# The lower levels of a block inverse in 32x32 tiles of the array, and FP4 weights decoded by their bits

## Time and profile before

| | us |
|---|---|
| three runs | 4791.87, 4797.97, 4799.29 (median 4797.97) |
| the profiled execution | 4795.44 |
| its span | 4793.6 |
| TensorE busy | 4570.4 (95%) |
| VectorE (DVE) busy | 3585.9 (75%) |
| ScalarE (ACT) busy | 2307.5 (48%) |
| POOL busy | 514.6 (11%) |

### The profile page before, as it was taken

One profiled execution on the slowest core, in us unless ns is written; L12 is line 12 of the kernel. 1 busy time (PEld: TensorE's weight loads), 2 busy tenths in 40 slices (PEclk: granted clock), 3 DMA queues, 4 the chain that ended last, 5 costly groups with the idle time before them and its releaser, 6 DMA issues. The chain is left out here.

```text
span 4793.6 us, 61029 instructions
## 1 busy us (share of the span) xinstructions
PE 4570.4 (95%) x20341; PEld 2909.4 (61%) x20341; DVE 3585.9 (75%) x8682; ACT 2307.5 (48%) x4841; POOL 514.6 (11%) x381
## 2 busy tenths in 40 slices
PE   7899999999999999999999999998577999999899
PEld 4677777677777677777677777667333444444343
DVE  5777777777777777777777777776475988988861
ACT  4455454555554555554554554553223554555433
POOL 1111111111111111111111111111010000000000
PEclk9999999999999999999999999999889999999999
DMA  2010110111100111100110100100200444444420
GB/s 75 31 34 32 35 33 27 34 32 29 38 30 27 34 33 58 43 29 27 34 34 27 38 29 27 34 27 10 83 1 18 161 144 136 156 145 145 150 90 18
DMA packets 202330, 262.10 MB, mean 55 GB/s; under 512 B 18174, under 2 KB 101378, under 8 KB 202018
## 3 DMA queue, kind: packets, MB, share of 16 engines
q1 hardware_dynamic: 202018, 258.20, 16.9%
HBM read 249.24 MB, written 8.91 MB: 54 GB/s over the span
## 5 line engine op out<-in xcount | busy, mean ns | idle before, releaser
L436 PE MATMUL bank<-xnT,w_qkv 128*128 128x512 f32 x2048 | 925.1, 594 | 4.1 <-ACT raw L720 3.4
L436 PEld LDWEIGHTS bank<-xnT,w_qkv 128*128 128x128 f32 x2048 | 373.5, 191 | 401.9 <-issue 383.2
L1004 DVE SCALAR_TENSOR_TENSOR conv<-raw,conv_w,conv 128x1024 f32<-128x1024 f32 x384 | 496.1, 1292 | 154.8 <-ACT conv L694 145.7
L547 PE MATMUL bank<-w_out_unit,oT 128*128 128x512 f32 x1024 | 497.1, 608 | 7.9 <-ACT oT L760 7.9
L508 PE MATMUL bank<-w_z_unit,xnT 128*128 128x256 f32 x2048 | 486.8, 381 | 0.0
L508 PEld LDWEIGHTS bank<-w_z_unit,xnT 128*128 128x128 f32 x2048 | 371.2, 191 | 41.2 <-issue 1.0
L791 ACT ACTIVATE squares<-o 128x128 f32<-128x128 f32 x512 | 153.9, 301 | 454.9 <-DVE o L1048 392.8
L1211 PE MATMUL bank<-xnT_f,w_gu 128*128 128x512 f32 x704 | 345.7, 637 | 11.1 <-PEq L1536 7.0
L1219 PE MATMUL bank<-xnT_f,w_gu 128*128 128x512 f32 x704 | 318.2, 595 | 0.0
L1229 PE MATMUL bank<-w_down,hidden 128*128 128x512 f32 x704 | 316.7, 593 | 1.1 <-DVE x_blocks L1271 1.1
L1103 POOL TENSOR_TENSOR inv<-n_base,block_mask 128x1024 f32<-128x1024 f32 x64 | 150.5, 2352 | 1422.2 <-DVE n_base L851 1422.2
(11 more groups left out here) (219 smaller groups left out, 8510.4 us busy)
## 6 DMA issues: line engine op xcount, KB each, us to landing
rows_b<-bc_rows SPq DMA_DIRECT2D x256, 256.0 KB, 3.3
rows_c<-bc_rows SPq DMA_DIRECT2D x256, 256.0 KB, 3.4
w_qkv<-in_w_qkv SPq DMA_DIRECT2D x128, 256.0 KB, 2.8
decay<-gc_rows SPq DMA_DIRECT2D x64, 512.0 KB, 3.9
w_z_unit<-in_w_z SPq DMA_DIRECT2D x32, 512.0 KB, 4.4
w_out_unit<-in_w_out SPq DMA_DIRECT2D x32, 512.0 KB, 5.0
x_after<-x SPq DMA_DIRECT2D x16, 256.0 KB, 2.0
x_blocks<-x_after SPq DMA_DIRECT2D x4, 1024.0 KB, 12.3
```

The source lines that it names most:

```text
L436: made = e.matmul(PROJ[:, :], w_qkv[:, p % 2, j, :], xnT[:, n // HK, j, h * BANK:(h + 1) * BANK], start=j == 0, stop=j == KT - 1)
L547: made = e.matmul(OB[:, :], oT[:, r, :], w_out[:, N % 2, r, :], start=r == 0, stop=r == REP - 1)
L1004: e.scalar_tensor_tensor(acc, raw[:, i % 2, tap:tap + T], conv_w[:, tap, col:col + 1], acc, ALU.mult, ALU.add).then_inc(on["conv"], 1)
```

## The change

The constants: the two masks `neg_mask` are gone; `slot_mask` (128 x 64) and `neg_odd` are made from `block_mask` by DVE.

`inv` is kept by rows of 64: a row of a matrix holds only the 64 columns of its own half (for rows 0 to 63 the columns 0 to 63, for rows 64 to 127 the columns 64 to 127). POOL's spread is 128 x 512. A tile `inv_turned` of the same shape holds the transposed squares before level 0.

```diff
+                for i in range(NC):
+                    if level == 0:
+                        for b in range(4):
+                            q, s = slice(32 * b, 32 * b + 32), 32 * (b % 2)
+                            if part == 0:
+                                made = e.matmul(evens_ps[q, i, :, :], lt[q, i, q], evens[q, i, :, :],
+                                                start=True, stop=True)
+                            else:
+                                made = e.matmul(tile_ps[q, i, :], inv_turned[q, i, s:s + 32], off[q, i, 0:32],
+                                                start=True, stop=True)
+                    elif level == 1:
+                        for b in range(2):
+                            up, low = slice(64 * b, 64 * b + 32), slice(64 * b + 32, 64 * b + 64)
+                            if part == 0:
+                                made = e.matmul(tile_ps[low, i, :], lt[up, i, low], inv[up, i, 0:32],
+                                                start=True, stop=True)
+                            else:
+                                made = e.matmul(tile_ps[up, i, :], off[low, i, 0:32], ttT[low, i, low],
+                                                start=True, stop=True)
+                        if part == 1:
+                            low = slice(32, 64)
+                            made = e.matmul(tile_ps[low, i, :], ttT[low, i, low], off[low, i, 0:32],
+                                            start=True, stop=True)
```

Level 2 keeps its 64 x 64 tiles. Part 0 of level 0 now waits for POOL's mask and not for DVE's transpose. DVE's side:

```diff
-            def turn_inverse(N, a):
-                ttT = invT_i(a)
-                e.transpose(ttT.rearrange("p n w -> p (n w)"), inv[:, :, :].rearrange("p n w -> p (n w)")).then_inc(
-                    on["inv_dve"], 1)
+            def turn_base():
+                e.transpose(inv_turned[:, :, :].rearrange("p n w -> p (n w)"),
+                            inv[:, :, :].rearrange("p n w -> p (n w)")).then_inc(on["inv_dve"], 1)
+
+            def turn_inverse(a):
+                for q in (slice(0, hp), slice(hp, P)):
+                    e.transpose(invT_i(a)[q, :, q], inv[q, :, :]).then_inc(on["inv_dve"], 1)
...
-                            mask = c["neg_mask"][16 << level][:, :].unsqueeze(1).broadcast_to([P, NC, P // 2])
-                            e.tensor_tensor(off[:, :, :], inv_ps, mask, ALU.mult).then_inc(on["inv_dve"], 1)
+                            sign = c["neg_odd"][:, 0:1] if level == 0 else -1.0
+                            e.tensor_scalar(off[:, :, 0:32], tile_ps, sign, None, ALU.mult).then_inc(on["inv_dve"], 1)
...
                             if level == 0:
+                                e.tensor_tensor(evens, evens_ps, evens, ALU.add).then_inc(on["inv_dve"], 1)
                                 e.wait_ge(on["inv_dve"], INV_STEPS * H + 3)
-                                turn_inverse(N, a)
+                                if n >= 1:
+                                    e.wait_ge(on["u_pe"], 8 * (n - 1) + HALF * a + HALF)
+                                turn_inverse(a)
                             else:
-                                e.wait_ge(on["inv_dve"], INV_STEPS * H + 6)
+                                e.tensor_copy(inv[32:64, :, 0:32], tile_ps[32:64, :, :]).then_inc(on["inv_dve"], 1)
                                 for q in (0, 64):
-                                    e.transpose(ttT[q:q + 32, :, q + 32:q + 64],
-                                                inv[q + 32:q + 64, :, q:q + 32]).then_inc(on["inv_dve"], 1)
+                                    e.tensor_copy(invT_i(a)[q:q + 32, :, q + 32:q + 64], tile_ps[q:q + 32, :, :]).then_inc(
+                                        on["inv_dve"], 1)
```

```diff
-                        e.tensor_scalar(spread[:, :, j], words, 4 * j, 15, ALU.logical_shift_right,
-                                        ALU.bitwise_and).then_inc(on["unpacked"], 1)
+                        e.tensor_scalar(spread[:, :, j], words, 4 * (NIB - 1 - j), 6, ALU.logical_shift_left,
+                                        ALU.arith_shift_right).then_inc(on["unpacked"], 1)
...
+                    e.tensor_scalar(bits, bits, FLOAT_BITS, None, ALU.bitwise_and).then_inc(on["unpacked"], 1)
                     e.wait_ge(on["unpacked"], done + NIB + 1)
...
+                    e.tensor_tensor(values.rearrange("p (g w) -> p g w", g=ng),
+                                    bits.bitcast(F32).rearrange("p (g w) -> p g w", g=ng),
+                                    by.unsqueeze(2).broadcast_to([P, ng, P]), ALU.mult).then_inc(on["unpacked"], 1)
```

```diff
+        def beside(i, place):
+
+            ahead = [("piece", k) for k in pieces_before(i + 1)] if i + 1 < IT else []
+            return (ahead[0:1], ahead[1:2], ahead[2:] + state_space[2 * (i - 2):2 * (i - 1)] if i >= 2 else ahead[2:])[place]
```

More of the change, by code:

```diff
@@ L149 @@
     gate x_add
-    pad select k_weight mask square o_scaled
+    pad inv_zero select k_weight mask square o_scaled
 """
@@ L347, in inverse @@
                 H = 2 * N + a
[L348 to L353, removed]
-                    else:
[L355 to L373, removed]
@@ new lines, in inverse @@
+                lt, ttT = lT_i[:, NC * a:NC * (a + 1), :], invT_i(a)
+                if level == 0 and part == 0:
+                    e.wait_ge(on["mask"], H + 1)
+                    if H > 0:
+                        e.wait_ge(on["invT"], H)
+                elif level < 2:
+                    e.wait_ge(on["inv_dve"], INV_STEPS * H + ((0, 2), (3, 6))[level][part])
+                elif part == 0:
+                    e.wait_ge(on["inv_dve"], INV_STEPS * H + 9)
+                else:
+                    e.wait_ge(on["inv_neg"], H + 1)
@@ new lines, in inverse @@
+                for i in range(NC):
[14 more added lines that the diff above has]
+                                                start=True, stop=True)
+                            else:
+                                made = e.matmul(tile_ps[up, i, :], off[low, i, 0:32], ttT[low, i, low],
[4 more added lines that the diff above has]
+                                            start=True, stop=True)
+                    elif part == 0:
+                        made = e.matmul(inv_ps[hp:P, i, :], lt[0:hp, i, hp:P], inv[0:hp, i, :],
+                                        start=True, stop=True)
+                    else:
+                        made = e.matmul(inv_ps[0:hp, i, :], off[hp:P, i, :], ttT[hp:P, i, hp:P],
+                                        start=True, stop=True)
@@ L1083, in gpsimd @@
             e.memset(raw[:, :, 0:PAD], 0.0).then_inc(on["pad"], 1)
+            e.memset(invT[:, :, :, 0:hp].rearrange("p c r w -> p (c r) w"), 0.0).then_inc(on["inv_zero"], 1)
             for slot in range(ATTENTION_SLOTS):
@@ L1137 @@
 BLOCKS = B * NH
+FLOAT_BITS = -0x7E400000
+HALF_POWER = 2.0 ** 63
 TILES = BANK // P
@@ L1315, in second_half @@
         order = [k for i in range(IT) for k in pieces_before(i)]
+        state_space = [("small", 0), ("dt_rows", 0)]
+        state_space += [("dt_w", i) for i in range(KT)] + [("out_w", i) for i in range(KT)]
+        def beside(i, place):
+            ahead = [("piece", k) for k in pieces_before(i + 1)] if i + 1 < IT else []
+            return (ahead[0:1], ahead[1:2], ahead[2:] + state_space[2 * (i - 2):2 * (i - 1)] if i >= 2 else ahead[2:])[place]
         prep = [("scale", 0), ("scale", 1)] + [("turn0", t) for t in range(TILES)]
-        prep += [("piece", k) for k in pieces_before(0)] + [("small", 0), ("dt_rows", 0)]
-        prep += [("dt_w", i) for i in range(KT)] + [("out_w", i) for i in range(KT)]
-        prep += [("piece", k) for i in range(1, IT) for k in pieces_before(i)] + [("turn1", t) for t in range(TILES)]
+        prep += [("piece", k) for k in pieces_before(0)]
+        prep += [use for i in range(IT) for place in range(3) for use in beside(i, place)]
+        prep += [("turn1", t) for t in range(TILES)]
         prep_at = {use: k for k, use in enumerate(prep)}
@@ L1398, in prepare @@
                         ng = piece(i)[1]
-                        e.wait_ge(on["scaled"], order.index(i) + 1)
+                        e.wait_ge(on["unpacked"], UNPACK_STEPS * (order.index(i) + 1))
                         values = val[:, order.index(i) % 2, 0:ng * P].rearrange("p (g w) -> p g w", g=ng)
@@ L1455, in scalar @@
                     evict(("turn0", t))
+                for k in pieces_before(0):
+                    evict(("piece", k))
                 for i in range(IT):
-                    for k in pieces_before(i):
-                        evict(("piece", k))
+                    for use in beside(i, 0):
+                        evict(use)
                     silu_gate(e, 0, i)
-                    if i == 0:
-                        for use in prep[prep_at[("small", 0)]:prep_at[("out_w", KT - 1)] + 1]:
-                            evict(use)
+                    if i == 2:
                         e.wait_ge(on["ss_params"], 48)
```

(17 more changed lines are left out.)

96 lines of the change are left out of this document (41 added, 55 removed).

## The result

The changed kernel takes 4494.0 us (median of four, 4491.8 to 4494.4) where the kernel before takes 4795.3; the ratio is 0.937, 95% interval 0.9354 to 0.9387. The forecast was 4720 with a range of 4550 to 4860: the program is faster, as was forecast, but the gain is 301 us where 75 were forecast. The profiled execution took 4493.6 us.

What follows compares the result with a forecast made beforehand. TensorE's record spacing was taken to bound the attention, DVE and the wait for POOL the FFN unpacking. Attention -42 + 52 - 5 = +5 us and unpacking -82 took 4795.4 to 4718, forecast as 4720 us, range 4550 to 4860.

Steps and rivals of the forecast that it cites:

- The bounds: Mid-attention: TensorE's record count and spacing, DVE relief worth nothing; FFN unpacking: DVE and TensorE's wait for POOL, longest 68.7 us.
- The spacing of a pair: Levels 0 and 1 of the inverse: 0.031 us per 32-column load and MATMUL, 208 pairs a half, saving 42 us.
- two rows that agree: Straight line through 128- and 64-column loads gives 0.031 us; two successive 32-column loads lie 0.03 us apart.
- -42: Inverse's records: 64 x 0.111 = 7.1 us a half becomes 208 x 0.031 = 6.45, over 64 halves.
- the way out's 28 of the 52: Leaving the tiles, 0.14 us more in the trace, within 256 excursions at 0.205 us, 52 us.
- Rival B: Inverse's tiles overlap more than assumed; at 0.0155 us a pair 206 us less, 4514; at 0.024, 4627; chance 0.27.
- Rival A: Tiled groups' spacing has a floor; slower above 0.037 us a pair; skill's 50 ns gives 4973 us; chance 0.17.
- Changing the tile size: Four more excursions into tiles a half in levels 0 and 1, 256 at 0.205 us: 52 us; ends 0 and 77.
- What lies beside: DVE's part of a half falls from 6.1 to 4.0 us, POOL's mask halves; priced at nothing beside a never-waiting TensorE.
- The start-up's 5 us: TensorE's 11.1 us wait for line 856's transpose at the start shrinks, 5 us gained; ends 0 and 11.
- The unpacking: FFN weights: a DVE piece falls from 5.49 to 2.15 us, TensorE then paces units at 11.8 us; gain 82 us.

Runs made afterwards that it cites:

- the probe: Kernel before plus sections of 32 matmuls (64 load/MATMUL pairs) on TensorE after the first transposes: 0.032 us a pair for one 32x32 tile, 0.016 two, 0.009 four.

## Why the prediction was wrong

**The bounds** were read rightly: TensorE's spacing in the attention, DVE and POOL in the unpacking. That the two stages can be costed apart was right too (-221 and -79 alone, -301 together). But the attention was forecast to lose 5 us and gained 217; that the whole came out faster, as forecast, is due in the forecast to the unpacking alone.

**The spacing of a pair is the step that failed.** "I take 0.031", "because it is nearest to two rows that agree": those rows all have every load in the same tile, and for one tile the probe confirms them (0.032). But level 0 goes round four tiles (0.009 us a pair), level 1 round two in part 0 (0.016) and three in part 1 (0.011). Summed from start to start in the trace, the tiled groups of levels 0 and 1 with their way out take 172 us, where the four groups of before took 456: -284, where the same terms of the prediction (-42, and the way out's 28 of the 52) come to about -14. Rival B named the mechanism, and its evidence against, that "two loads in succession never lie closer than 0.03", was the same rows of one tile again. B was also mis-sized: it priced two abreast for all pairs, and in level 0 four go abreast. At the measured spacings its 206 us would be 273. That its 4514 lies near 4494 is partly luck: the wait for u (28 us) and the dearer change of size (12 us) took back most of what the third and fourth tile gave. At 0.27 it was held too unlikely, and the range ended at 4550, inside it.

**Rival A** is refuted as priced: the floor exists, but at 0.009 us, far below the 0.037 from which it would decide. Its 50 ns were also worked out at 1.2 GHz, where the granted clock in the middle was 1.00, the 2.4 GHz level; half of it, 25 ns, is still far above the 9 measured.

**Changing the tile size** was right as far as it was counted: 0.09 in and, for line 369, 0.69 - 64 x 0.009 = 0.11 out, 0.20 for 0.205. What was not counted: the first record behind a tiled group lasts 0.048 us longer up to the next start than it did behind the 128x128 groups of before (lines 320, 552, 568; for line 568 0.533 for 0.485). That makes 0.25, the price that the probe has, and 64 us in place of 52.

**What lies beside** was priced at nothing with TensorE as the cover. It was only part right. The cover itself shrank: a part in front of line 552 went from 1.81 to 0.69 us, and the wait for ScalarE's u, which in the middle of the attention held up only weight loads before (12 us), now stops the matmuls too. The prediction named the eviction between the parts on DVE and missed that on ScalarE, which costs some 35 us. DVE's part of a half is 4.7 us, not 4.0: the 64x512 transposes take 0.706 and the copies 0.417. The start-up's 5 us were right: the idle time before the first part went from 11.1 to 6.5 us.

**The unpacking** was right in size and cause: -82 forecast, -81 in the trace, -79 alone. Some 18 of the 81 us are clock given back. Before, the gate matmuls behind TensorE's wait for a piece took 4.65 to 6.19 us in units 0 to 9 (granted clock 0.59 in one of 5.96). After, units 0 and 1 take 5.59 and 5.24, and the others 3.60. The same 704 records on the two pages:

```profile
L1211 PE MATMUL bank<-xnT_f,w_gu 128*128 128x512 f32 x704 | 345.7, 637 | 11.1 <-PEq L1536 7.0
...
L1237 PE MATMUL bank<-xnT_f,w_gu 128*128 128x512 f32 x704 | 327.6, 609 | 11.1 <-PEq L1560 7.0
```

**Sum,** from start to start in both traces: -284 for the groups; +21 in the records before them (lines 529 and 556), which is the way in; +12 in the first records behind them, 0.048 us for each of 256; +28 at line 320 for u (156.2 us for 125.0, less the 3 already counted); and +5 spread over unchanged records, whose cause is open: -218 for the 217 measured.

## What to carry to other kernels

A spacing that is read from loads into one tile says nothing about loads into several. Before a price is put on tiled matmuls, note the order in which the tiles take turns; if no row has two in turn, both ends belong in the range. When the bounding engine gets faster at one place, list each wait behind that place on every other engine, and how long the removed work had covered it; a transfer or table load that stood there for free becomes the next term. If it is moved, look at the next waited-for instruction behind its new place, and at the granted clock behind each new wait.

## What the runs showed of the hardware

- Float32 pairs of load and MATMUL in different tiles overlap, within a group of rows, of columns, or on the diagonal: 0.032, 0.016, 0.009 us for one, two, four tiles, and 0.009 for sixteen. The Trainium skill (TensorE: Matmul & The Clock Gate, Part 3: Packing small matmuls — row/col tiling) says that a load overlaps with a running matmul only when the group of rows differs; here four tiles in one group of rows were as fast as four on the diagonal (0.75 us for 64 pairs), and the measurement decides.
- A split of the array's columns pays also for full-height matmuls where the load sets the pace: 0.056 us for what takes 0.111 in the probe, and 134 us in the whole kernel.
- Single matmuls of 32x32 and 128x128 in turn cost 0.25 us a round beside their own pairs (0.54 for 0.29), at a granted clock of 1.00.
- In that alternating section (141.18 to 151.9), which stands behind wide matmuls, the profile shows TensorE busy without a break. The granted clock was 1.00, the 2.4 GHz level, up to 146 and then 0.50, the 1.2 GHz level, to the section's end and some 4 us into the wide matmuls behind it; a round takes 0.86 us there, where it takes 0.54 before (columns: stretch, us, PE busy, PEld busy, the others, granted clock; the second row is the mean of both levels):

```profile
141.00:146.00 5.00, 5.00 (x37) 3.87 (x36) 0.00 (x0) 0.00 (x0) 0.00 (x0) 1.00 0.00 0
146.00:157.00 11.00, 11.00 (x36) 6.91 (x36) 0.00 (x0) 0.00 (x0) 0.00 (x0) 0.54 0.01 1
```

In the changed kernel, where wide matmuls stand between the tiled groups, the middle stretch keeps 1.00.
